# One core, a graph layer with attention and two experts: matrix products in quarters of the array and a new division of work in the attention stage

## What is computed

```python
# edge part: only the first 6250 edges of (dst, src) are read
xt = x @ weight                                  # 4 heads of 64
alpha = softmax(leaky_relu(xt[dst] . attn_l + xt[src] . attn_r))
edge = sum over heads of alpha * xt              # repeated 4 times

# attention part, one position per row, so each convolution is its middle tap
h = batchnorm(h @ w_qkv); t = relu(h)            # 768 channels, 8 groups of (q, k, v) of 32
s = pointwise(depthwise(t))                      # 32 x 32 per block of 32 channels
t2 = [t, s] scaled by its norm
out = v * sum(k) * q, divided by v + 1e-15       # per group; k, q after relu
fx = scale(out @ w_res + b_res)

# two experts chosen by the mean of all rows, gelu, then a layer norm
```

## Time and profile before

| | |
|---|---|
| median of 3 runs | 925.59 us (923.23 to 926.26) |
| profiled execution, its own time | 925.73 us |
| its span, first to last instruction | 923.8 us |
| mean granted TensorE clock | 0.960 |
| busy: TensorE, VectorE, ScalarE, POOL | 824.0, 553.8, 399.4, 416.1 us |
| rows and xt | to 84 us |
| pre-activations | 84 to 211 us |
| attention with its tail | 211 to 562 us |
| experts | 562 to 924 us |

### The profile page before, as it was taken

How to read it: one execution, slowest core, us unless ns; L and a number is a source line. 1 busy time by engine, 2 the same in 40 slices (tenths; PEclk the granted TensorE clock), 3 DMA queues, 4 the chain that set the end, 5 groups by cost and what they waited for, 6 DMA issues and landing times. The chain is left out here.

```text
span 923.8 us, 13742 instructions
## 1 busy us (share of the span) xinstructions
PE 824.0 (89%) x4438; PEld 696.1 (75%) x4438; DVE 553.8 (60%) x1617; ACT 399.4 (43%) x819; POOL 416.1 (45%) x652
## 2 busy tenths in 40 slices
PE   4889999997779898989857867999999999999992
PEld 3678888884567677777646656888888888888882
DVE  6663687876667887887888853234434343344444
ACT  2465433345677776767636413232223223223220
POOL 2321888882367676666644650033133223223224
PEclk9999999997999999999988977999999999999997
DMA  8744222220011111111110004000000000000001
GB/s 198 186 142 127 49 58 51 52 58 18 15 54 41 32 38 34 36 38 35 38 35 15 28 5 114 0 23 12 23 23 13 22 23 17 19 23 20 15 23 33
DMA packets 35099, 41.22 MB, mean 45 GB/s; under 512 B 11329, under 2 KB 20255, under 8 KB 35023
## 3 DMA queue, kind: packets, MB, share of 16 engines
q1 hardware_dynamic: 22743, 30.71, 11.8%
q0 software_dynamic: 8000, 6.82, 3.3%
q10 hardware_dynamic: 4280, 2.79, 1.3%
HBM read 25.59 MB, written 14.60 MB: 44 GB/s over the span
## 5 line engine op out<-in xcount | busy, mean ns | idle before, releaser
L854 ACT ACTIVATE Z<-ps,b1s 128x250 f32<-128x250 f32 x200 | 94.0, 470 | 236.1 <-PE ps L1064 236.1
L1064 PE MATMUL ps<-Z 128*128 128x250 f32 x800 | 175.6, 377 | 2.4 <-DMA b1s<-in_b 2.4
L1077 PE MATMUL ps<-Z 128*125 128x256 f32 x800 | 176.5, 379 | 0.0
L1064 PEld LDWEIGHTS ps<-Z 128*128 128x128 f32 x800 | 153.1, 192 | 21.1 <-issue 2.8
L1077 PEld LDWEIGHTS ps<-Z 128*125 128x125 f32 x800 | 150.0, 187 | 22.4
L916 PE MATMUL ps<-Z,L 128*128 128x250 f32 x600 | 126.9, 373 | 0.0
L641 POOL TENSOR_SCALAR zr<-zmv 125x2 f32<-125x2 f32 x25 | 5.5, 220 | 265.8 <-issue 216.2
L916 PEld LDWEIGHTS ps<-Z,L 128*128 128x128 f32 x600 | 113.6, 189 | 13.2
L936 PE MATMUL ps<-Z,pw 128*128 128x250 f32 x300 | 84.2, 404 | 21.3 <-DVEq L1464 19.1
L1645 DVE TENSOR_TENSOR Z<-ps,L 125x256 f32<-125x256 f32 x50 | 21.2, 425 | 120.0 <-PE ps L1077 119.9
L998 PE MATMUL ps<-wr,Z 128*125 128x256 f32 x400 | 92.8, 386 | 0.0
(11 more groups left out here) (212 smaller groups left out, 1313.9 us busy)
## 6 DMA issues: line engine op xcount, KB each, us to landing
Z<-in_x SPq DMA_DIRECT2D x25, 250.0 KB
out<-Z SPq DMA_DIRECT2D x25, 250.0 KB
xt_table<-L SPq DMA_DIRECT2D x25, 231.0 KB
Z<-in_x SPq DMA_DIRECT2D x1, 2016.0 KB
g_table<-gt SPq DMA_DIRECT2D x25, 62.5 KB
gr<-g_table SPq DMA_DIRECT2D x25, 62.5 KB
Z<-in_x SPq DMA_DIRECT2D x1, 1344.0 KB
Z<-in_x SPq DMA_DIRECT2D x1, 1120.0 KB
```

What stands on the lines that cost most here:

```text
L854: a_.activation(ge[:, b % 2, f, :], ps[:, f % 4, 0:BT], ACT.Gelu, bias=b1s[:, f // NF, f % NF:f % NF + 1]).then_inc(gelu_done.sem, 1)
L1064: last = mm(ps[:, f % 4, 0:BT], w1s[:, f // NF, k, (f % NF) * 128:(f % NF + 1) * 128], h_of(b, k), start=(k == 0), stop=(k == KD - 1))
L1077: last = mm(ps[0:TP, 4 + 2 * (b % 2) + t, 0:D], ge[:, b % 2, f, t * TP:(t + 1) * TP], w2s[:, f // NF, f % NF, :], start=(f == 0), stop=(f ...
```

## The change

- **Quarters.** `quarter` makes one product of 64 rows by 64 columns of the array. Q, V and the K sums of s use the quarters (0,0) and (1,1), rows before columns. K and the K sums of t use (0,1) and (1,0), which swaps the two halves of K's channels in s; the order of K's channels in Z, in `pw` and in the batch norm's values (`q ^ 2`) is swapped to fit. K and Q become one stage (`pointwise_kq`), V and the K sums of t another (`pointwise_v`).
- **ReLU.** The relu of K of all 25 blocks is done at n = 30 to 54 of the pre-activations, that of Q of blocks 0 to 19 at n = 55 to 74, the rest of Q and all of V in the attention stage. `bn_affine` comes at b = 3 instead of 13, `bn_power` after gathers 6 and 13 instead of 8 and 14.
- **Division of work.** `keep_norms` and `keep_xn` go from VectorE to ScalarE. The clamp of the norms goes from POOL to `keep_turned` on VectorE, as a second operand of the copy that it replaces; POOL's L569 is dropped.
- **Order.** See the lists. Both statistics of x1 are issued between the read of the flag and the branch, their aggregation after it. The work for a late block is spread over three steps.
- **Division.** Where the flag asks for it, fewer of its instructions wait for the one before, and the two halves use separate buffers.

```diff
-        WQ_IN, BN_IN, PW_IN, LATE = 16 * KD, 16 * 3, 16 * 8, 16 * 3
+        WQ_IN, BN_IN, PW_IN, LATE = 16 * KD, 16 * 3, 16 * 16, 16 * 3
...
+        EARLY_RELU, EARLY_Q = 30, 20
...
-            return i if i < AHEAD else PIECES * (i - AHEAD) + PIECES + 2
+            return 3 * i if i < AHEAD else PIECES * (i - AHEAD) + PIECES + 2
...
-                    if b == (8, 14)[kind]:
+                    if b == (6, 13)[kind]:
                         bn_power(kind)
...
-                    act.dma_start(pw[32 * q:32 * q + 32, h:NC:NH, 32 * q:32 * q + 32], pw_v[h, q]).then_inc(pw_in, 16)
+                    act.dma_start(pw[32 * q:32 * q + 32, h:NC:2 * NH, 32 * q:32 * q + 32], pw_v[h, q][:, 0:3:2]).then_inc(pw_in, 16)
+                    p = q ^ 2
+                    act.dma_start(pw[32 * p:32 * p + 32, 2 * R_K + h, 32 * p:32 * p + 32], pw_v[h, q][:, R_K]).then_inc(pw_in, 16)
...
-                i = n - (3 * NB - 6)
+                i = n - EARLY_RELU
                 if i == 0:
+                    act.wait_ge(bn_done.sem, bn_done.count(0))
+                if i == NB:
                     act.wait_ge(bn_done.sem, bn_done.count(1))
-                if 0 <= i < RELU_Q:
-                    relu(0, i)
+                if 0 <= i < NB:
+                    relu(i, R_K, relu_k)
+                if i >= NB:
+                    relu(i - NB, R_Q, relu_q)
...
+            def quarter(to, lhsT, rhs, a, e):
+
+                rows_, cols_ = slice(HALF * a, HALF * a + HALF), slice(HALF * e, HALF * e + HALF)
+                return mm(to[cols_], lhsT[rows_, HALF * a:HALF * a + HALF], rhs[rows_], start=True, stop=True)
...
+            def pointwise_kq(b):
+                pe.wait_ge(relu_k.sem, relu_k.count(b))
+                pe.wait_ge(relu_q.sem, relu_q.count(b))
+                if b:
+                    pe.wait_ge(s_sq.sem, s_sq.count(b - 1))
...
+                for h in range(NH):
+                    cq, ck = 2 * R_Q + h, 2 * R_K + h
+                    for a in range(2):
+                        quarter(bank_half(R_Q, h), pw[:, cq, :], zc(b, cq), a, a)
+                        last = quarter(bank_half(R_K, h), pw[:, ck, :], zc(b, ck), a, 1 - a)
+                last.then_inc(s_done.sem, 1)
+
+            def pointwise_v(b):
+
+                pe.wait_ge(relu_v.sem, relu_v.count(b))
                 if b:
+                    pe.wait_ge(fixed.sem, fixed.count(b - 1))
                     pe.wait_ge(att.sem, att.count(b - 1, 1))
...
                 for h in range(NH):
+                    cv, ck = 2 * R_V + h, 2 * R_K + h
+                    for a in range(2):
+                        last_v = quarter(bank_half(R_V, h), pw[:, cv, :], zc(b, cv), a, a)
+                        last_k = quarter(bank_half(3, h), bo, zc(b, ck), a, 1 - a)
+                last_v.then_inc(s_done.sem, 1)
+                last_k.then_inc(kst_done.sem, 1)
...
-                    last = mm(ps[:, 4, h * BT:(h + 1) * BT], bo[:], skr[:, h * BT:(h + 1) * BT], start=True, stop=True)
+                    for a in range(2):
+                        last = quarter(bank_half(4, h), bo, skr[:, h * BT:(h + 1) * BT], a, a)
...
             steps(NB, [
-                (0, lambda b: pointwise(b, R_K, RELU_K)),
-                (0, k_sums_t),
+                (0, pointwise_kq),
+                (4, turn_xn),
                 (1, turn_norms),
-                (0, lambda b: pointwise(b, R_Q, RELU_Q)),
-                (4, turn_xn),
                 (2, res),
-                (0, lambda b: pointwise(b, R_V, RELU_V)),
+                (0, pointwise_v),
                 (0, k_sums_s),
                 (0, norms),
             ])
```

VectorE's list, the flag and the branch:

```diff
-            def divide_where_needed(b):
+            def divide_where_needed(b, meanwhile):
...
                 found = dve.value_load(flag[0:1, a, 1:2].bitcast(I32), min_val=0, max_val=ONE)
+                meanwhile()
...
+            def branch(b):
+                divide_where_needed(b, lambda: sums_of_x1(b - 2) if b >= 2 else None)
...
             steps(NB, [
-                (1, keep_norms),
+                (1, check_s),
                 (0, keep_k),
+                (0, check_t),
                 (1, keep_turned),
                 (3, make_x1),
-                (3, sums_of_x1),
-                (1, divide_where_needed),
-                (0, attend_t),
+                (1, branch),
+                (3, moments_of_x1),
                 (2, make_u),
                 (3, make_xn),
-                (4, keep_xn),
+                (0, attend_t),
                 (0, attend_s),
-                (0, check_t),
-                (0, check_s),
-                (0, rest_now),
-                (0, logits_now),
+                (0, late_now),
             ])
```

More of the change, by code:

```diff
@@ L321, in gps_layer @@
         o_sq = stage("o_sq", 1)
-        checked = stage("checked", 3)
+        checked = stage("checked", 2)
+        raw_checked = stage("raw_checked", 1)
         att = stage("att", 3)
@@ L330, in gps_layer @@
         slow = sem("slow")
-        scale_n = stage("scale_n", 4)
+        scale_n = stage("scale_n", 3)
         se_done = stage("se_done", 1)
@@ L772, in keep_q @@
             def keep_q(b):
[L773 removed]
+                act.wait_ge(s_done.sem, s_done.count(b, S_KQ))
                 if b:
@@ L809, in late_softmax, with keep_norms @@
                         a_.activation(at[0:TP, 4, 0:TB], at[0:TP, 3, 0:TB], ACT.Exp).then_inc(late_exp.sem, 1)
+            def keep_norms(b):
+                act.wait_ge(norm_done.sem, norm_done.count(b))
+                if b:
+                    act.wait_ge(conv_done.sem, conv_done.count(b - 1))
+                else:
+                    act.wait_ge(nsb_clear, 1)
+                qs = slice(0, 128 if b else 96)
+                a_.activation(nsb[qs, :], ps[qs, 5, 0:BT], ACT.Copy).then_inc(norm_kept.sem, 1)
@@ L811, in _, with keep_xn @@
+            def keep_xn(b):
+                act.wait_ge(xn_turned.sem, xn_turned.count(b))
+                for k in range(KD):
+                    a_.activation(h_of(b, k), ps[:, 7, k * BT:(k + 1) * BT], ACT.Copy,
+                                  accum_out=rsum[:, k, b:b + 1]).then_inc(xn_kept.sem, 1)
             act.wait_ge(bn_done.sem, bn_done.count(2))
-            for i in range(RELU_Q, RELU_V):
-                relu(0, i)
+            relu(0, R_V, relu_v)
             square_t(0)
-            real = lambda f: lambda b: f(b) if b < NB else None
@@ L816, in _ @@
-            ahead = lambda i: lambda b: relu(b + 1, i) if b + 1 < NB else None
-            pipeline(0, NB, [
-                (0, ahead(0)),
-                (0, ahead(1)),
+            ahead = lambda f: lambda b: f(b + 1) if b + 1 < NB else None
+            steps(NB, [
+                (1, keep_norms),
+                (3, tanh),
                 (0, late_softmax),
-                (3, tanh),
-                (0, ahead(2)),
-                (0, ahead(3)),
-                (0, ahead(4)),
+                (0, lambda b: square_s(b, R_Q)),
@@ L825, in _ @@
                 (0, keep_q),
-                (0, lambda b: square_s(b, R_Q, S_Q)),
-                (0, lambda b: square_s(b, R_K, S_K)),
+                (0, lambda b: square_s(b, R_K)),
+                (4, keep_xn),
+                (0, ahead(lambda b: relu(b, R_Q, relu_q) if b >= EARLY_Q else None)),
+                (0, ahead(lambda b: relu(b, R_V, relu_v))),
                 (1, square_o),
-                (0, ahead(5)),
-                (0, lambda b: square_t(b + 1) if b + 1 < NB else None),
@@ L831, in _ @@
-                (0, lambda b: square_s(b, R_V, S_V)),
+                (0, lambda b: square_s(b, R_V)),
                 (2, square_u),
+                (0, ahead(square_t)),
             ])
+            keep_norms(NB - 1)
+            tanh(NB - 3)
+            keep_xn(NB - 4)
+            square_o(NB - 1)
+            square_u(NB - 2)
+            keep_norms(NB)
+            tanh(NB - 2)
+            square_u(NB - 1)
+            keep_xn(NB - 3)
+            tanh(NB - 1)
             act.wait_ge(rt_dve, RT_EXP)
@@ L1313, in late_rest, with late_sum @@
                     ALU.mult).then_inc(e.sem, 1)
+            def late_sum(i):
+                e, a = late, i % 2
                 dve.wait_ge(e.sem, e.count(i, 8))
@@ L1362, in _ @@
                         edge_sums(p)
-                if kind and b == 13:
+                if kind and b == 3:
                     bn_affine(kind - 1)
@@ L1510, in logits_now, with late_now @@
+            def late_now(s):
                 for i in range(NB - EARLY):
-                    if s == edge_step(i):
-                        late_logits(i)
-            def rest_now(s):
-                for i in range(NB - EARLY):
-                    if s == edge_step(i) + 1:
-                        late_rest(i)
+                    for after, part in enumerate((late_logits, late_product, late_sum)):
+                        if s == edge_step(i) + after:
+                            part(i)
@@ L1540, in _ @@
             ])
```

(12 more changed lines are left out.)

155 lines of the change are left out of this document (73 added, 82 removed).

## The result

| | before | after |
|---|---|---|
| median of 4 runs | 925.65 us (923.23 to 926.26) | **895.63 us** (893.01 to 896.25) |
| profiled execution, its span | 925.73, 923.8 us | 893.01, 891.2 us |

A forecast was written before the change was run, and what follows sets the result against it. VectorE's in-order list was taken as the bound, TensorE just behind. Savings of 20 + 3.8 + 3.8 + 1.5 and half a us for the tail, 29.6, took 925.7 to 896 us; 8-in-10 range 883 to 913.

The forecast's parts named there:

- The step of 9.87: VectorE's attention step without edge work: 9.47 us of list plus 0.4 waiting for rstd, down from 10.77.
- 9.47: VectorE's step: 10.77 us less keep_norms 0.33, keep_xn 0.67 and the 0.30 wait for the turned norms.
- 0.4 taken: VectorE at make_xn: a new wait for POOL's rstd, 0.2 to 0.6 us a step, paid in full.
- 5.0 us off each group of four: The 16 middle attention steps: four steps plus 3.05 us late edge work, 42.5 against 47.5; 20 us in all.
- The same end as before: VectorE's flag read and branch: with statistics behind the read, the section ends at 329.9 as before, so no gain.
- my bound of +0.5: VectorE's branch section: bounds of -0.6 and +0.5 us around the neutral estimate for the new place of the statistics.
- 0.6 was taken as the read: VectorE's 1.08 us of flag read and branch: the read's share, between 0 and 1.08, taken as 0.6.
- Four side by side: TensorE's quarter products: all four quarters run at once, pairs take 2.55 us instead of 4.25, TensorE 8.7 a step.
- Both engines have to be relieved, or nothing comes of it: Attention stage: TensorE stands just behind VectorE's 10.77 us step, so relieving only one of them would gain nothing.
- TensorE's 10.4 us: TensorE's attention step before: pairs 4.25, res 3.4, norms 1.7 and turns about 1.05 us, together 10.4.
- I credited 3.8 us: The five steps ahead of the 16: three gain 1.25 us each, two waiting for gr's DMA gain nothing.
- 3.8 for three steps, 1.5 for the division and 0.5 for the tail: Behind the 16 steps: savings from three steps, cheaper division copies with fewer waits, and keep_norms no longer behind the tail's checks.

The follow-up runs named there:

- experiment 7: Also written f_sums_first: the kernel after with the statistics of x1 ahead of the flag read on VectorE; 884.7 us, 0.957 of the kernel before.
- (12): The kernel before with only the evictions of the norms and of the turned x moved to ScalarE; 912.82 us, 0.9864.
- (1): The kernel after with the quarters undone, all five pairs as whole 128x128 products again; 897.74 us, 0.9728 of the kernel before.
- (3): The kernel after with ReLU of K and Q back in the attention stage for all blocks but the first; 896.97 us, 0.970.
- (11): The kernel after with whole products, ReLU of K and Q late, and statistics of x1 ahead of the flag read; 899.15 us, 0.9716.
- experiment 2: The kernel after with the evictions of the norms and of the turned x back on VectorE; 915.65 us, 0.9912 of the kernel before.
- h_small_edge: The kernel after with POOL's add_edge on 8 of 64 columns of each head, the rest left out; 870.48 us, 0.9417.
- g_edge_later: The kernel after with add_edge behind scale_of_u in POOL's order; 891.99 us, 0.965 of the kernel before.
- d_xn_later: The kernel after with make_xn behind attend_t in VectorE's order; 882.69 us, 0.9544 of the kernel before.

## Why the prediction was right, and where it was not

**The step.** VectorE's list in order is the cycle, and the evictions and the wait for the turned norms left it as forecast. The step of 9.87 came out at 9.8 to 10.02, in part by errors that cancel. In the step shown, against 9.47: the branch section +0.19 (2.95 us became 3.14; zero was taken), make_xn +0.40 (1.08 us became 1.48, not forecast at all; one of the two operations was slow in that step of before already, 0.43 and 0.81 us, and the mean went from 0.48 in the same stretch of before to 0.82), rstd +0.20 (0.4 taken), and -0.23 of small gaps between the checks. The sum is 10.03; the start to start distance of attend_t is 10.08.

Over the 16 steps the cancelling is larger, and it is luck. The prediction took 5.0 us off each group of four, but its step accounts for 3.6 (0.9 each). The other 1.4 came in without a term: the groups of before stood 4.4 us above four steps of 10.77, and only the 3.05 of edge work was put back. VectorE from keep_k to keep_k, 16 steps of each trace (190.2 us from 278.02, 170.2 us from 269.63); a row counts from the start of an operation to the start of the next, with waits in rows of their own:

| us in 16 steps | before | after | difference | forecast |
|---|---|---|---|---|
| the two evictions | 16.1 | 0 | -16.1 | -16.0 |
| wait for the turned norms | 4.6 | 0.6 | -4.0 | -4.8 |
| make_xn | 12.9 | 23.8 | +10.9 | none |
| wait for rstd | 0 | 3.4 | +3.4 | +6.4 |
| make_u | 20.0 | 16.6 | -3.4 | none |
| waits in make_u, mostly for res | 4.7 | 1.6 | -3.1 | none |
| waits for the scale at make_x1 | 2.6 | 0.3 | -2.3 | none |
| late edge work | 11.7 | 12.3 | +0.6 | 0 |
| all else, mostly gaps around the checks | 117.6 | 111.6 | -6.0 | none |

The groups behind it (mean ns; before from 273 to 450 us, after from 266 to 428), se, make_xn and the rest of make_u:

```profile
L1471 DVE SCALAR_TENSOR_TENSOR se<-npw,cc 125x2 f32<-125x2 f32 x15 | 7.2, 480 | 0.0
L1500 DVE TENSOR_SCALAR L<-Z,mv,rstd 125x256 f32<-125x256 f32 x30 | 13.1, 478 | 0.0
L1478 DVE SCALAR_TENSOR_TENSOR L<-ps,se,brow 125x256 f32<-125x256 f32 x30 | 13.1, 479 | 4.3 <-PE ps L998 3.2
```
```profile
L1528 DVE SCALAR_TENSOR_TENSOR se<-npw,cc 125x2 f32<-125x2 f32 x15 | 2.4, 161 | 0.0
L1559 DVE TENSOR_SCALAR L<-Z,mv,rstd 125x256 f32<-125x256 f32 x31 | 24.3, 823 | 3.0 <-POOL rstd L619 3.0
```

So the new lists took se out from beside add_edge and put make_xn, which is larger, beside it in every step. The two longest waits for res in before, 1.89 and 0.82 us, fall in the two steps with a mean clock of 0.86. Four savings that were not forecast stand against one cost that was not.

**The branch.** "The same end as before" was nearly right for the step and wrong as a judgement of the part: experiment 7 puts it at 10 us for the kernel and 0.26 us for each of the 16 steps, inside my bound of +0.5. The term that failed is the share of 1.08 us that work behind the read could hide: 0.6 was taken as the read, and in the change 1.11 us pass before the statistics start.

**The quarters.** Four side by side, as taken. "Both engines have to be relieved, or nothing comes of it" fell: VectorE alone gives 12.6 us (12) and everything but the quarters 25 (1). TensorE's 10.4 us is 10.56 by its own cycle, and it is a floor only once the rest is below it.

**ScalarE.** It covers its new work. The pre-activations lag by nothing; the evictions and relus cost nothing in the middle. The relus' real worth lies in the first five steps, where I credited 3.8 us and 5.4 came: with the relus left late the same five steps take 56.4 us (3) and 55.7 (11), with them early 51.9 in the change and 48.6 to 53.8 in the other runs. In the medians experiment 3 loses only 1.3 us, within noise. Only one of the two waits for gr is left (4.80 us).

**Behind the 16 steps.** I gave 3.8 for three steps, 1.5 for the division and 0.5 for the tail, 5.8 in all; the trace has 0.3 in the step of the division, 1.3 in the two behind it and 4.2 in the tail, again 5.8. The division's own run of operations fell by 1.67 us (16.57 to 14.90, the 16 copies from 4.54 to 3.44), but a late sum of 1.04 us now falls into that step. The step after it begins with 1.71 us in which VectorE waits for TensorE, and takes 10.9 us with the clock at a mean of 0.91. The tail was mis-sized. From attend_t of the last block to its nrm VectorE took 7.30 us (524.71 to 532.01) and now takes 3.42 (495.52 to 498.94), since make_u, make_xn and keep_xn of older blocks no longer stand in between. With the evictions back that stretch is 4.58 (515.72 to 520.30).

**Stage 1** is 2.3 us shorter in the trace and not by the change as far as any run here shows; the experiments' first square_t starts between 213.1 and 216.3 us, and the medians differ by 30.0 us where the traces differ by 32.6.

## What to carry to other kernels

When one engine's list in order is the cycle, moving 1 us off it is worth about 1 us a step where nothing else is close (the steps without edge work in experiment 2) and less where another bound is (0.56 us a step in experiment 12). For the same edit the gains were 5 or 8, and 12.6 or 20, depending on what else had been done. Before and after a re-ordering, look at the durations as well as the waits. Here the operation that waited for POOL's rstd started in step with POOL's next one, and an operation of VectorE on SBUF alone, even one of 125x2, took longer beside it. Where a line of before had records of two durations, POOL's addition ran beside the long ones, so the price could be read ahead of the change. Work that should cover the making of a flag belongs ahead of its read; behind the read it covered nothing here.

## What was not expected of the hardware

- make_xn on VectorE, all operands in SBUF, takes 0.41 us per operation alone or beside a small addition (h_small_edge) and 0.82 in step with POOL's addition of 125x256. POOL's goes from 0.75 (g_edge_later) to 0.93 in d_xn_later, where it meets both a 128x500 SBUF addition and make_xn. VectorE's 128x500 addition on SBUF alone went from 0.68 to 0.79 there, its 125x2 se from 0.15 to 0.70 in before. An operation with an operand in PSUM kept its 0.67 us.
- Two row halves of TensorE write one PSUM bank in different partitions at full rate, 0.21 us from one round of four records with 250 columns to the next.
- The read of a flag and the branch kept VectorE idle for 1.07 to 1.46 us after its last operation in the middle steps of before, with the flag ready 0.7 us or more ahead of that operation's end. In the change the next operation starts 0.85 to 0.87 us after the flag (325.42 to 326.27), in f_sums_first 1.14 to 1.54 us after it and 0.71 to 1.13 us after the last operation. What decides between these values no run shows.
